# First mixture of experts: the router's logits turned round, four column tiles at a time

## The reference

```python
logits = jnp.einsum('btd,ed->bte', x, gate_w)            # 8 logits per row
top_val, top_idx = jax.lax.top_k(logits, 2)
top_w = jax.nn.softmax(top_val, axis=-1)
y_all = jnp.einsum('btd,edm->btem', x, We)                # 8 experts, 128 -> 128
out = jnp.sum(take_along_axis(y_all, top_idx) * top_w)    # the best two, weighted
...
x = x + jnp.tanh(g_ffn[0]) * _L0_ffn_ref(_layernorm(x, axis=-1), L0_ffn_gate_w, L0_ffn_We)
```

## Time and profile before

| | |
|---|---|
| time, median of 3 runs | 2160.76 us (2160.32 to 2162.66) |
| the profiled execution | 2156.8 us, span 2155.0 us |
| mean granted TensorE clock | 0.947 |
| PE busy | 1918.2 us, 89% of the span |
| DVE busy | 1670.9 us, 78% |
| ACT busy | 1297.6 us, 60% |
| first statistics of the first mixture to its last update L958 | 612.69 to 783.95 us |

### The profile page before, as it was taken

The page is one execution under the profiler, slowest core; times in us unless marked ns, Lnnn a source line. Parts: engine busy times, 40 slices in busy tenths (PEclk is TensorE's granted clock), DMA queues, the critical chain, the costliest instruction groups (busy, mean ns, idle before and its releaser), DMA issues. The chain is left out here.

```text
span 2155.0 us, 48493 instructions
## 1 busy us (share of the span) xinstructions
PE 1918.2 (89%) x17841; PEld 1473.2 (68%) x17841; DVE 1670.9 (78%) x4752; ACT 1297.6 (60%) x3151; POOL 263.6 (12%) x551
## 2 busy tenths in 40 slices
PE   7999999999969999999999797999999994699608
PEld 6777787787759987777767575777677773344208
DVE  6787787787759979999867797667766488787894
ACT  5777777777742238888866464444455265218744
POOL 1111111111111111111111241000000022100000
PEclk9999999999969999999999898999999997799859
DMA  5222221111125621111100111222222110002452
GB/s 156 52 65 59 53 57 46 44 46 42 42 99 222 237 94 33 33 32 32 24 1 1 30 50 79 80 103 95 79 79 80 50 50 21 0 0 103 179 187 79
DMA packets 115148, 151.60 MB, mean 70 GB/s; under 512 B 45657, under 2 KB 96354, under 8 KB 110818
## 3 DMA queue, kind: packets, MB, share of 16 engines
q1 hardware_dynamic: 111730, 146.91, 21.1%
q10 hardware_dynamic: 3184, 1.58, 0.3%
HBM read 110.18 MB, written 21.50 MB: 61 GB/s over the span
## 5 line engine op out<-in xcount | busy, mean ns | idle before, releaser
L1808 ACT ACTIVATE arena<-banks,b1c 128x512 f32<-128x512 f32 x192 | 131.9, 687 | 166.4 <-PE banks L1645 166.2
L1736 DVE TENSOR_TENSOR arena<-arena 128x512 f32<-128x512 f32 (+1 forms) x256 | 170.5, 686 | 61.5 <-ACT arena L1808 56.4
L624 ACT ACTIVATE arena<-banks,arena 128x128 f32<-128x128 f32 x512 | 180.6, 373 | 1.3 <-DVE arena L570 1.3
L1655 PEld LDWEIGHTS banks<-w2a,arena 128*128 128x128 f32 x1024 | 124.1, 192 | 28.7 <-issue 28.7
L496 PE MATMUL banks<-arena,wk 128*128 128x128 f32 x1024 | 134.0, 285 | 1.2 <-DVE arena L594 1.2
L876 PE MATMUL banks<-we,arena 128*128 128x128 f32 x1024 | 131.5, 285 | 1.5 <-DVE arena L947 0.2
L535 PE MATMUL banks<-wv,arena 128*128 128x512 f32 x256 | 131.9, 597 | 0.0
L496 PEld LDWEIGHTS banks<-arena,wk 128*128 128x128 f32 x1024 | 121.7, 195 | 12.5 <-issue 10.8
L876 PEld LDWEIGHTS banks<-we,arena 128*128 128x128 f32 x1024 | 122.8, 197 | 7.0 <-DVE arena L947 6.2
L1655 PE MATMUL banks<-w2a,arena 128*128 128x128 f32 x1024 | 124.7, 275 | 0.0
L541 PEld LDWEIGHTS banks<-konst,arena 128*128 128x128 f32 x512 | 59.1, 141 | 93.6 <-DVE arena L552 59.0
(11 more groups left out here) (246 smaller groups left out, 5023.5 us busy)
## 6 DMA issues: line engine op xcount, KB each, us to landing
arena<-coef_scratch SPq DMA_DIRECT2D x32, 2048.0 KB, 7.2
arena<-arena SPq DMA_DIRECT2D x256, 64.0 KB, 2.0
gated_scratch<-arena SPq DMA_DIRECT2D x16, 768.0 KB, 3.3
arena<-gated_scratch SPq DMA_DIRECT2D x16, 768.0 KB, 4.4
arena<-z1T_scratch SPq DMA_DIRECT2D x128, 64.0 KB, 2.3
arena<-in_ctx_turned SPq DMA_DIRECT2D x32, 256.0 KB, 2.9
arena<-in_ctx SPq DMA_DIRECT2D x64, 64.0 KB, 2.1
z1T_scratch<-arena SPq DMA_DIRECT2D x64, 64.0 KB, 1.6
```

The source lines that it names most:

```text
L624: act.activation(prob[:, o, c * P:(c + 1) * P], ps[:, SCORES + o, c * P:(c + 1) * P], ACT.Exp, bias=low[:, o, c:c + 1], accum_out=total[:, ...
L1655: mm = pe.matmul(ps[:, OUT + g.par, j * D:(j + 1) * D], hT[g.par][:, c, j * P:(j + 1) * P], w, start=c == 0, stop=c == CHUNKS2 - 1)
L1736: dve.tensor_tensor(hT[g.par][rows, c, :], hT[g.par][rows, c, :], wide_coef[g.par][rows, e, :], ALU.mult).then_inc(s["scaled"].sem, 1)
L1808: act.activation(hT[g.par][:, c, :], ps[:, HID + c % NHID, :], ACT.Gelu, bias=k.b1c[:, c:c + 1])\
```

## The change

The operands of the logits' matmuls are exchanged. wg_roomy is a new stationary operand of 128 x 32, zero but for the router's eight columns, filled once at the head of DVE's part of the stage (a memset and a copy). Tile j uses the 32 columns of the array from 32 j (a column tile) and writes 32 partitions of PSUM; xT of the tile moves, 128 columns. So the logits come out turned: expert e of tile j on partition 32 j + e. ACT copies the 128 x 128 block to SBUF (logitsT) as the first thing of its step, ahead of the copy of the coefficients; PE turns it with one transpose, placed between the second and third quarters of the outputs, and only this signals l_psum. DVE then copies the same 32 logits, now 8 of every 32 columns. In steps without outputs the transpose stands right behind the matmuls.

```diff
--- before.py
+++ after.py
@@ -832,9 +832,12 @@
     coef = [k.take(GROUP * EXPERTS) for _ in range(2)]
     coefT = [k.take(P) for _ in range(2)]
     shift = k.take(GROUP)
+    ROOM = P // GROUP
+    wg_roomy, logitsT = k.take(ROOM), k.take(P)
+    cleared = k.sem("L0_cleared")
     COLS = GROUP * EXPERTS
     XT, LOGITS, COEFT, OUT = 0, 1, 2, 3
-    s = k.sigs(G, dict(shift=1, l_psum=1, l_sb=1, gap=1, share=2, part=1, coef=1, ct_psum=1, ct_sb=1, scaled=EXPERTS,
+    s = k.sigs(G, dict(shift=1, lt_psum=1, lt_sb=1, l_psum=1, l_sb=1, gap=1, share=2, part=1, coef=1, ct_psum=1, ct_sb=1, scaled=EXPERTS,
                        out_psum=1))
     coef_dram = k.nc.dram_tensor("coef0_scratch", [G, COLS, P], F32, kind="Internal").ap()
     coef_stored, coef_spread = k.transfers(G, "coef_stored"), k.transfers(G, "coef_spread")
@@ -877,6 +880,8 @@
                                k.we0[:, n, :], start=n == 0, stop=n == EXPERTS - 1)
             if j == GROUP - 1:
                 mm.then_inc(s["out_psum"].sem, 1)
+
+        pe.wait_ge(cleared, 2)
 
         def body(at):
             if g := at(0):
@@ -891,11 +896,16 @@
                 if g.has(1):
                     pe.wait_ge(*s["l_sb"](g.back(1)))
                 for j in range(GROUP):
-                    mm = pe.matmul(ps[:, LOGITS, j * EXPERTS:(j + 1) * EXPERTS], xT[g.idx % LIVE][:, j * P:(j + 1) * P],
-                                   k.wg0[:, :], start=True, stop=True)
-                mm.then_inc(s["l_psum"].sem, 1)
+                    mm = pe.matmul(ps[j * ROOM:(j + 1) * ROOM, LOGITS, 0:P], wg_roomy,
+                                   xT[g.idx % LIVE][:, j * P:(j + 1) * P], start=True, stop=True)
+                mm.then_inc(s["lt_psum"].sem, 1)
             if g := at(0):
-                for j in range(1, GROUP):
+                outputs(g, 1)
+            if g := at(3):
+                pe.wait_ge(*s["lt_sb"](g))
+                pe.transpose(ps[:, LOGITS, P:2 * P], logitsT, k.ident).then_inc(s["l_psum"].sem, 1)
+            if g := at(0):
+                for j in range(2, GROUP):
                     outputs(g, j)
             if g := at(4):
                 pe.wait_ge(*f["xhat_ready"](sub(g, GROUP - 1)))
@@ -907,11 +917,15 @@
         unrolled(G, 4, 0, body)
 
     def vector(dve):
+        dve.memset(wg_roomy, 0.0).then_inc(cleared, 1)
+        dve.wait_ge(cleared, 1)
+        dve.tensor_copy(wg_roomy[:, 0:EXPERTS], k.wg0[:, :]).then_inc(cleared, 1)
+
         def top_two(g):
             dve.wait_ge(*s["l_psum"](g))
             if g.has(1):
                 dve.wait_ge(*s["part"](g.back(1)))
-            dve.tensor_copy(route.score, ps[:, LOGITS, 0:COLS].rearrange("p (j e) -> p j e", j=GROUP))\
+            dve.tensor_copy(route.score, ps[:, LOGITS, P:2 * P].rearrange("p (j e) -> p j e", j=GROUP)[:, :, 0:EXPERTS])\
                 .then_inc(s["l_sb"].sem, 1)
             dve.wait_ge(*s["l_sb"](g))
             k.hold(dve)
@@ -981,6 +995,9 @@
                 act.activation(share[:, n], gap, ACT.Sigmoid, scale=2.0 * n - 1.0).then_inc(s["share"].sem, 1)
 
         def body(at):
+            if g := at(3):
+                act.wait_ge(*s["lt_psum"](g))
+                act.activation(logitsT, ps[:, LOGITS, 0:P], ACT.Copy).then_inc(s["lt_sb"].sem, 1)
             if g := at(2):
                 act.wait_ge(*s["ct_psum"](g))
                 if g.has(2):
```

## The result

The changed kernel takes 2177.95 us in the median of 7 runs (2172.34 to 2183.2), the kernel before 2162.66 (2157.95 to 2169.06) in the same comparison. The ratio of the two is 1.0065, with a 95% interval from 1.005 to 1.008: 14 us slower (11 to 17); the medians differ by 15.3. The prediction said 2176.5, between 2171 and 2183.

A forecast was written before the change was run, and what follows sets the result against it. The prediction took DVE to pace the stage, with PE close behind. Head 0.65, lateness by step 1 2.4, steps 2 to 11 11.2 and step 12 1.5 make 15.8 us; median 2160.76 becomes 2176.5, range 2171 to 2183.

The forecast's parts named there:

- The bound: First mixture's steps: DVE sets the pace and PE is close behind; period 9.24 us.
- The logits' matmuls: PE's block of eight records on column tiles: 0.40 us in place of 0.82, bounds 0.24 and 0.91.
- The place of the signal: Signal behind the second quarter: PE's path 3.01 us replaces DVE's 1.86, period 10.36; 11.2 us over steps 2 to 11.
- W: Point in each step where DVE ends a group's last scaling (L947); DVE's own path from there to L914 is 1.86 us.
- Head and step 0: Head of the stage 0.65 us late, bounds 0.2 and 2; in step 0, at low clock, L914 2.8 us late.
- What stands beside the path: Copy of the coefficients delayed, store and spread move 0.6 us; slack 2 us and more, so no cost.
- Step 12: L914 comes 10.36 us behind the one before in place of 8.83: 1.5 us more.
- The tail: From step 13 on there are no logits; PE's last 176 records move as a whole, adding nothing.
- A: Tiles run one after the other: block 0.91 us, 6.1 us more over 12 steps, 2182.7 us; chance 0.07.
- B: PE paces and the late signal doesn't matter: 0.31 us gained in each of 13 steps, 2156.8 us; chance 0.05.
- C: Granted clock stays at the lower level as PE idles: PE's step some 16.3 us, total 2246 us; chance 0.03.
- D: Something, such as a shorter DVE path behind L914, covers most of the stall: less than 4 us left, 2163; chance 0.02.

The follow-up runs named there:

- the late place alone: Kernel before the change, with only the eight old logits' records moved behind the second quarter of the outputs: 2182.7 us, ratio 1.0096.
- ACT's copy: Kernel before the change, old logits in their old place, ACT instead of DVE copying the logits out of PSUM: ratio 0.9985, run again 0.9976.
- POOL's scaling with the old logits: Kernel before the change, with ACT copying the old logits and POOL making the eighth scaling of every group: 2162.23 us, ratio 1.0003.
- one-tile kernel: Changed kernel with all four groups of logits' matmuls on the first 32 array columns, leaving out three tiles' logits in four: one run, 2192.84 us.
- the turn at once: Changed kernel with the logits' transpose straight behind their matmuls, ahead of the second quarter: 2161.07 us, ratio 0.9996.
- DVE's other order: Changed kernel, PE's list untouched, DVE reordered: three scalings ahead of the routing, two between it and the coefficients, three behind: 2164.07 us, ratio 1.0011.

## Why the prediction was right

**The bound.** Right: DVE paces, and PE has 0.47 us a step to spare (its weight loads wait 0.17 and 0.31 for L947 in the kernel before). Shown from both sides, by the late place alone (slower with PE's work unchanged) and by ACT's copy (faster with PE's work unchanged).

**The logits' matmuls.** Forecast 0.40 us from start to start, measured 0.36 (740.18 to 740.54). The 0.16 in that forecast doesn't follow from the 0.23 and 0.22 beside it; it is what 16 x 0.029 leaves of the 0.62 us from the start of the 16 records of the earlier trace rows to the start of what follows (1233.03 to 1233.65). And from the turn of the coefficients to the block it is 0.20 and not 0.11 (739.98 to 740.18), which I had left out.

**The place of the signal.** Forecast 3.01 us from W, measured 3.14. Per period the loss is 10.50 - 9.21 = 1.29 in place of 1.15. Over the ten periods from step 1 to 11 it is 105.30 us in place of 92.37: 12.9, forecast 11.2. This is the term that I undersized: by 0.09 a period ahead of the block, by 0.08 in the second quarter (740.54 to 742.43 is 1.89, forecast 1.81; its first record takes 0.21 to the next start where the others take 0.11, as it took 0.19 behind the old logits), less the 0.04 of the block; and by 0.3 once, because one period in ten is some 0.3 longer in both traces (731.89 to 742.74 after), which I had counted for the kernel before alone.

**Head and step 0.** Forecast 0.65 for the head, measured none: L928 in step -3 comes 9.12 us behind L601, L914 came 9.24 behind it. The memset and the copy delayed the statistics by 0.2. But from the first record of the logits to DVE's copy it is 1.57 us (622.37 to 623.94) where it was 1.91 (619.63 to 621.54): at the low clock the old block took 1.87 to its last end, the tiles take 0.65, and that pays for copy and turn. The prediction had the logits of this step 0.25 late. From there step 0 is 2.3 late (forecast 2.8): its quarter took 2.91 us and not 16 x 0.22 = 3.5, since the granted clock rose in it (0.50 from 644 to 646 us, 1.00 from 647). Step 1 makes up 0.3 (10.49 behind step 0, before 10.79). By step 1 the sum is 1.9, forecast 3.05.

**What stands beside the path.** The spread is issued 2.93 us from W where it was 2.42 (742.53, and 746.94 in the earlier trace rows): 0.5 later, forecast 0.6, and no L961 from 655.97 to 765 us waits for it. PE's waits for the scalings grew to 1.0 us a step (11.2 over 11), not to 1.9; another 0.7 is its new wait for the normalised rows, which the prediction didn't name. It is not on the way from W to L928.

**Step 12.** 10.50 in place of 8.83: 1.7, forecast 1.5.

**The tail.** Forecast nothing, measured 0.8. The prediction let PE's last 176 records move as a whole. In both kernels the end hangs on the last spreads: DVE's last eight scalings start 0.08 us behind the landing of theirs, and the last update 10.9 behind their start. The wait of 1.86 us ahead of the eight scalings before them, at 765.03, is of the same kind; it is the one wait of DVE that the prediction's reading of the waits passed over. Before:

```profile
765.14 0.32 SPq L856 DMA_DIRECT2D arena<-coef_scratch  x1
...
772.28 4.91 DVE L947 TENSOR_TENSOR arena<-arena 128x512 f32<-128x512 f32 x8 [1.68 <-issue]
```

After, the spread is issued at 783.89 and the scalings start at 792.09. From the copy of step 12 to the issue it is 0.27 less than before (9.66 and 9.93), and the spread takes 8.12 us where it took 7.06: 0.8 in all. In the four kernels with the old logits in their old place (the one before, the two runs with ACT's copy alone, and POOL's scaling with the old logits) this last spread takes 7.06 to 7.39 us, in the eight others 7.91 to 9.10 (taken over all traces of this document). So the tail's 0.8 seems to belong to the change; why the same transfer takes longer there, no run shows.

The sum is -0.1 + 2.3 - 0.3 + 12.9 + 1.7 + 0.8 = 17.3 for the stage, where the prediction had 15.8; its errors (0.8 and 0.4 too much by step 1, 1.7 too little in the periods, 0.2 and 0.8 after them) partly cancel, and that the total comes so near is in part luck. The ratio of whole times gives 11 to 17.

**The rivals.** A (tiles one after the other): not so, the block takes 0.36 us to the quarter's start and 0.99 in the one-tile kernel. B (PE paces, faster): not so, the kernel is slower, and PE's saving brought nothing with the turn at once either. C (the clock falls): the granted clock stayed at 1.00 although PE was busy for 82.78 of 90.03 us. D (something covers most of the stall): not so, DVE waits 1.19 us in every period.

## What to carry to other kernels

A pipelined stage has two paths from one landmark to the next: the pacing engine's own list, and the round trip through the other engine. In this stage work taken off the other engine gave nothing; a signal could be moved later there only by the slack between the two paths (0.4 us), and every tenth beyond it was paid in each period. An engine that shows 99% busy may still be the one that waits: read who waits for whom, then take one instruction off the suspected pacer and see whether the period follows.

## What was not expected of the hardware

- PE's weight loads stand idle 0.20 to 0.21 us ahead of a block of 32-column tiles and again behind it, with no releaser shown, at a granted clock of 1.00. PE itself shows no idle time there, for matmuls still run; 0.09 us ahead of the block is left in their starts. By the Trainium skill (TensorEngine Tiling (Array Packing), Key Properties) a change of tiling mode drains the engine; the trace agrees.
- Eight float32 records of 32 x 128 take 0.43 us to the last end on four column tiles and 1.06 on one.
- POOL's operation of 128x512 with two SBUF inputs (1.27 us) makes DVE's CAST of 128x8 take 0.87 us in the mean in place of 0.17, and in the kernel with DVE's other order POOL's L729 beside L961 takes 1.57 in five steps and 2.77 in two, in place of 1.01. By the Trainium skill (SBUF — State Buffer, SBUF: two separate sides) GpSimd shares one pair of ports with VectorE's instructions of two SBUF inputs or in a 2-port mode, and whoever starts first holds it for a whole instruction. Both rows agree, L961 with its two inputs plainly; that the CAST is in such a mode no run here shows, only that it ends when POOL's instruction does. A small instruction in a chain of dependent ones can thus give back all that moving a large one to POOL took away.
